# A wait for the landing of an earlier gather, ahead of every fourth gather of the relation sums

## The reference, cut to what matters

```python
hx = jnp.einsum('ni,rio->rno', x, weight)
msg = hx[edge_type, src]
agg = jax.ops.segment_sum(msg, dst, num_segments=num_nodes)
node_repr = agg * jnp.asarray(ALPHA, x.dtype) ** 0.5
node_repr = node_repr + h_bias
loop_message = x @ loop_weight
```

## Time and profile before

| | us |
|---|---|
| median of 3 runs | 5387.18 |
| profiled execution, its own time | 5382.89 |
| its span | 5381.2 |
| `relation_sums`, from its first gather to its last | 886.3 to 2431.4 |
| POOL busy over the span | 2949.7 (55%) |
| PE busy over the span | 3810.3 (71%) |
| DVE busy over the span | 2663.2 (49%) |

### The profile page before, as it was taken

One profiled execution on the slowest core, in us unless ns is written; L12 is line 12 of the kernel. 1 busy time (PEld: TensorE's weight loads), 2 busy tenths in 40 slices (PEclk: granted clock), 3 DMA queues, 4 the chain that ended last, 5 costly groups with the idle time before them and its releaser, 6 DMA issues. The chain is left out here.

```text
span 5381.2 us, 72918 instructions
## 1 busy us (share of the span) xinstructions
PE 3810.3 (71%) x19358; PEld 2805.5 (52%) x19383; DVE 2663.2 (49%) x9403; ACT 1683.5 (31%) x4007; POOL 2949.7 (55%) x2997
## 2 busy tenths in 40 slices
PE   4888886855456455546787778787757787777798
PEld 2454554633333333335566566565526666766566
DVE  7655532444435333326333333233895666666782
ACT  3434342222222222223333333333542222222330
POOL 5777766566667666662554545453265555555121
PEclk9999998877777777775888888888888999999798
DMA  6544444343333333332222122121638888988001
GB/s 223 163 154 160 157 161 133 95 120 89 91 89 89 90 91 89 95 94 49 56 46 47 41 47 50 39 49 44 217 126 291 293 294 295 310 305 289 14 1 48
DMA packets 351544, 690.80 MB, mean 128 GB/s; under 512 B 70241, under 2 KB 174062, under 8 KB 344779
## 3 DMA queue, kind: packets, MB, share of 16 engines
q0 software_dynamic: 139328, 355.39, 22.6%
q1 hardware_dynamic: 211821, 330.73, 18.7%
HBM read 573.52 MB, written 112.35 MB: 127 GB/s over the span
## 5 line engine op out<-in xcount | busy, mean ns | idle before, releaser
L1020 POOL DMA_INDIRECT e_ring<-table,erow x1040 | 1004.5, 966 | 541.9 <-issue 270.3
L1362 PE MATMUL e_sums<-e_ring,e_onehot 128*128 128x257 f32 x2080 | 753.5, 504 | 634.4 <-DVE e_onehot L1275 423.0
L2458 POOL DMA_INDIRECT t_source<-source_rows,t_index x632 | 599.2, 948 | 604.5 <-DVE t_parts L2544 400.5
L1362 PEld LDWEIGHTS e_sums<-e_ring,e_onehot 128*128 128x128 f32 x2080 | 407.1, 236 | 806.3 <-DVE e_onehot L1275 459.1
L1474 POOL DMA_INDIRECT e_ring<-table,esrc x544 | 529.8, 974 | 399.0 <-PE e_sums L1571 245.4
L554 POOL DMA_INDIRECT r_ring<-rows,esrc x528 | 584.9, 1108 | 236.2 <-issue 130.9
L998 ACT ACTIVATE k_sign<-ramp,low 128x128 bf16<-128x128 f32 x1024 | 352.4, 393 | 954.3 <-DMA r_xw<-rows 466.0
L2653 PE MATMUL t_out<-t_w,t_hidden 128*128 128x256 f32 x1600 | 449.4, 418 | 104.7 <-issue 101.9
L1559 PE MATMUL e_total<-e_loads,e_times 128*128 128x256 f32 x3072 | 520.1, 306 | 1.2 <-issue 1.2
L2642 PE MATMUL t_raw<-big,t_w 128*128 128x256 f32 x1600 | 441.7, 426 | 58.2 <-issue 40.5
L1235 DVE SCALAR_TENSOR_TENSOR big<-e_sums,within,big 128x257 f32 x130 | 63.0, 484 | 822.0 <-remote 697.0
(11 more groups left out here) (532 smaller groups left out, 6361.1 us busy)
## 6 DMA issues: line engine op xcount, KB each, us to landing
e_loads<-table SPq DMA_DIRECT2D x512, 256.0 KB
table<-r_stage SPq DMA_DIRECT2D x49, 1024.0 KB
outputs<-first_outputs SPq DMA_DIRECT2D x49, 512.0 KB, 6.6
first_outputs<-t_stage SPq DMA_DIRECT2D x96, 256.0 KB
t_near<-near_rows SPq DMA_DIRECT2D x79, 256.0 KB
e_ring<-table,erow POOLq DMA_INDIRECT x1040
table<-n_split SPq DMA_DIRECT2D x49, 256.0 KB
t_source<-source_rows,t_index POOLq DMA_INDIRECT x632
```

The source lines that it names most:

```text
L1020: eng.indirect_dma_start(ring[:, t % RING, 0:D], None, table, bass.IndirectOffsetOnAxis(ap=b.erow[:, EARLY + t:EARLY + t + 1], axis=0)).th ...
L1362: eng.matmul(sums[g % SUMS][:, 0:ACCW], onehot[t % ONEHOTS][:, :], ring[:, t % RING, :], start=(t % GROUP == 0), stop=(t % GROUP == GROUP ...
L2458: eng.indirect_dma_start(source[s][:, q, :], None, a.source_rows, bass.IndirectOffsetOnAxis(ap=index[s][:, q:q + 1], axis=0)).then_inc(gat ...
```

## The change

Ahead of tiles 4, 8, 12, ... GpSimd waits until the gather of two tiles back has landed (16 on its slot's `gathered`, counted by rounds of the ring), and adds one to `cleared`. There are 259 such waits. Nothing else is changed.

```diff
     SUMS = 2
+    PACE = 4
     SLOTS = (3, 10)
...
             for t in range(TILES):
                 if t >= RING:
                     eng.wait_ge(summed, t - RING + 1)
+                    eng.sem_inc(cleared, 1)
+                if t % PACE == 0 and t > 0:
+                    eng.wait_ge(gathered[(t - 2) % RING], 16 * ((t - 2) // RING + 1))
                     eng.sem_inc(cleared, 1)
                 eng.indirect_dma_start(ring[:, t % RING, 0:D], None, table, bass.IndirectOffsetOnAxis(
                     ap=b.erow[:, EARLY + t:EARLY + t + 1], axis=0)).then_inc(gathered[t % RING], 16)
```

## The result

The changed kernel takes 5458.56 us (median of four runs) where the kernel before takes 5387.32 us: a ratio of 1.0139, with an interval of 1.0093 to 1.0184. The forecast was 5370 us and faster, so it was wrong in sign; the number lies inside the range over both signs.

What follows compares the result with a forecast made beforehand. Bound: the relation sums' gathers, stalled by a full ring as TensorE's reports come late. Terms -19 - 10 + 12 = -17 us on 5382.9 give 5366, the median 4.3 above: 5370 (5340 to 5380; over both signs 5335 to 5490).

Steps and rivals of the forecast that it cites:

- The circle: Relation sums: in runs of gathers TensorE's semaphore reports come late and the ring fills; POOL stalls 3.6 us every 17 gathers.
- sets in 6.4 us into a run: Late TensorE reports were said to begin 6.4 us, five gathers, into an unbroken run, read from the attention phase.
- gather t starts at 2.4 + 0.78 = 3.2 us behind t - 2, 0.7 us late: Price of each new wait: landing 2.4 us after a gather's start, restart 0.78, against 2.50 in a free run.
- bounds of 0 and 0.8: Limits in us on how late one wait makes POOL's next gather, 0 if the landing is seen early enough.
- the forecast's 1.445: Paced rate in us a gather without any stall, against 1.466 before: 19 us less over 907 gathers.
- The first part: First 133 gathers of the relation sums: 10 us less expected if the late reports go, bounds 0 and 24.
- leftover spells: A few spells of late reports expected to remain, three at 4 us of stall: 12 us more.
- The rule on early waits: Issue DMAs early, wait late; by it the waits cost the waits-on-top price or at least 181 us of POOL's time.
- The waits on top: Rival: late reports and ring stalls stay and the waits add to them, 159 us more, 5545; chance 0.17.
- the stroke grows: Rival: pauses only delay the late reports, giving 24 gathers between stalls at 1.50 us each, 5410; chance 0.27.
- its own pause: The extra pause of 0.7 us ahead of every fourth gather that the forecast put into its sum.
- the forecast's 17 us less: Whole predicted gain on the profiled execution: -19 main part, -10 first part, +12 leftover spells; chance 0.42.

Runs made afterwards that it cites:

- paced260_again: The change's waits only up to tile 260, none for the other 780 tiles, on a chip with late TensorE reports: ratio 1.0008 to the kernel before.
- back3b: Waits ahead of every fourth gather as in the change, but for the gather three back instead of two: ratio 1.0019 to the kernel before.
- fill_long: Kernel before plus a GpSimd `tensor_scalar` over 208 columns into a scratch tile ahead of every fourth gather, no landing wait: ratio 1.0106.
- back6b: Waits ahead of every fourth gather as in the change, but for the gather six back instead of two: ratio 0.9976 to the kernel before.
- fill_mid: Kernel before plus a GpSimd `tensor_scalar` over 148 columns into a scratch tile ahead of every fourth gather, no landing wait: ratio 1.0028.

## Why the prediction was wrong

**The circle, and that the waits break it: right.** What was to be seen came: runs of four gathers, "remote" gone ahead of `add`, TensorE waiting for gathers at the lower clock, no late report in the main part. paced260_again, back3b and fill_long show by experiment that breaks in the gathers do it, and neither the sequencer's distance nor a backlog of TensorE. That it sets in 6.4 us into a run is true of the attention phase alone: it took some 12 us in paced260_again.

**The step that failed: "gather t starts at 2.4 + 0.78 = 3.2 us behind t - 2, 0.7 us late", and its bounds of 0 and 0.8.** The 0.78 held (0.75). The 2.4 was the end of the transfer's slices (the fourteenth, at 0 in those tenths, shows in the same view's GB/s row as 33); the semaphore is passed at 2.76. So a wait makes POOL 1.01 us late, above the upper bound, and the cycle is 6.01 us instead of 5.7 (6.03 in the median of the trace). That is 0.31 / 4 = 0.077 us a gather, 907 x 0.077 = 70 us. The kernel before had the right number where TensorE stood waiting for a gather that started at 1733.17:

```profile
1733.17 0.95 POOL L1020 DMA_INDIRECT e_ring<-table,erow  x1 [0.30 <-issue]
...
1736.03 0.67 PE L1362 MATMUL e_sums<-e_ring,e_onehot 128*128 128x257 f32 x2 [0.47 <-DMA e_ring<-table,erow]
```

2.86 us. So it is in 14 of the 24 tiles for which the profile says that it waited so (2.82 to 3.05; the other ten 3.5 to 5.1), and in no tile of the 1040 did the multiplication start less than 2.81 us behind its gather. A pause of 2.8 + 0.75 - 2.5 = 1.05 us would have given 6.05 / 4 + 0.02 = 1.53 a gather, 907 x 0.066 = 60 us more, 5447 us and "slower", from rows that were there.

**Left out: late landings.** Of the 226 waits behind tile 132, nine saw their landing more than 3.2 us after the start, 14 us too late in all. In a free run nobody notices; behind a wait POOL does. It is 0.015 us a gather. Both terms together are 84 of the 88 us between the forecast's 1.445 and the measured 1.542 (times 907).

**The first part and the leftover spells.** 214.4 us for what took 216.5, so 2 us less where the forecast had 10; no late spell was left, where it had 12 us. These two nearly offset each other. Added up the other way: 259 waits of 1.01 us are 262 us, and the stalls that went were worth 0.19 x 1040, some 200 us.

**The rule on early waits.** "DMA: Bandwidth & Descriptors" of the Trainium skill (rules for kernel authors) says to issue a DMA early and to wait on its semaphore late. The runs side with it, and the prediction gave it too little weight: back3b and back6b, whose waits are late enough, cost nothing, the change's cost 1.01 us each. By the fit in the same page of the Trainium skill (anatomy of one DMA) the prediction's estimate for this size is 2.3 us; the semaphore was passed at 2.76, 0.46 later.

**The rivals.** "The waits on top" (5545) is refuted, since the stalls went; "the stroke grows" (5410) had the right direction for a wrong reason, since no late report was left. Would the forecast have held with its own pause? fill_mid comes near it: it has 0.78 and no late reports in the main part, and its ratio is 1.0028. Taking away its longer gathers (0.027 us each, 28 us of 5400 or 0.5%) leaves 0.998, give or take 0.002. That is an estimate, and it can't tell the forecast's 17 us less (0.997) from no change. What it shows is how thin the forecast was: it set the rate without stalls only 0.02 below the circle's, and the tail of late landings alone took 0.015.

Open is what delays TensorE's reports in a run of gathers, and why two chips don't show it. Every run here worked from GpSimd's side, and every break thins out GpSimd's issuing and the transfers together, so no run tells which of the two matters.

## What to carry to other kernels

Read the price of a wait for a DMA from an engine that already waits for one of that kind, not from the transfer's own record. Before removing a stall by pacing, compare its mean cost per step with the pacing's, with the tail of late landings in it: here the stalls cost 0.19 us a gather and the waits 0.25 and 0.015 of tail, and a stall that an engine takes only when it must is cheaper than a wait that it always takes. And a gain that comes from breaking a chip's bad behaviour must be checked on a chip that doesn't behave so, where the same change is all cost.

## What the runs showed of the hardware

- The same program takes 5387 us on one chip and 4502 us on another. In the relation sums the difference is the stalls: 1.466 and 1.275 us a gather at an equal time for each gather. Phases without gathers take the same on both (180.3 us and 180.3).
- In an unbroken run of GpSimd's gathers, one each 1.25 us, TensorE's semaphore increments arrive up to 23.5 us late (VectorE's start behind the end of the multiplication) on most of the chips, with TensorE behind and with it two or three tiles behind the gathers. The rate at which gathers then go is 1.46 to 1.47 us in all of: rings of 8 and 19, waits that don't stop POOL, and a break of 0.10 us a gather.
- A gather's landing is passed by a waiting sequencer 2.76 us after the gather's start (median; 2.67 to 8.8 over two runs), and the next gather starts 0.75 us later.
- A 128x96 addition on GpSimd takes 0.353 us and is followed by a gap of 0.16 us, where a gather is followed by 0.30: short other work between two gathers costs less than its duration.
- A gather that starts while VectorE adds 128x1792 floats (2.0 us, L1265) takes up to 2.8 us instead of 0.95.
